# Graph attention on one core: the mask moves to the end, onto a word that holds both halves of a weight

## What is computed

```python
def _agnn(x, a, beta):
    x_norm = x / clip(norm(x, axis=-1), EPS)
    scores = beta[0] * (x_norm @ x_norm.T)
    scores = where(a > 0, scores, NEG_INF)
    attn = softmax(scores, axis=-1)
    return attn @ x

x = x + gnn(relu(layernorm(x)), adj, ...)
h = relu(layernorm(x))
h = leaky(_agnn(h, adj, beta1))
h = leaky(_agnn(h, adj, beta2))
out = x + h
```

## Time and profile before

| what | us |
|---|---|
| median of 3 runs | 1070.74 (1069.54 to 1072.2) |
| the profiled execution's own time | 1071.25 |
| its span, first to last instruction | 1069.7 |
| busy: TensorE, VectorE, ScalarE, GpSimd | 990.1, 929.9, 679.1, 34.0 |
| mean granted clock of TensorE | 0.972 of 2.4 GHz |

### The profile page before, as it was taken

One profiled execution on the slowest core, in us unless ns is written; L12 is line 12 of the kernel. 1 busy time (PEld: TensorE's weight loads), 2 busy tenths in 40 slices (PEclk: granted clock), 3 DMA queues, 4 the chain that ended last, 5 costly groups with the idle time before them and its releaser, 6 DMA issues.

```text
span 1069.7 us, 24266 instructions
## 1 busy us (share of the span) xinstructions
PE 990.1 (93%) x8672; PEld 665.3 (62%) x8672; DVE 929.9 (87%) x2276; ACT 679.1 (63%) x894; POOL 34.0 (3%) x31
## 2 busy tenths in 40 slices
PE   2889999999977699999999999969999999999995
PEld 2754444444445377777777777737777777777774
DVE  7692888888899979999999999958899899998996
ACT  2721112111234478889889898858888888888784
POOL 0000000000013500000000000000000000000000
PEclk9889999999998899999999999989999999999998
DMA  9228998888852346556555666616566665666600
GB/s 306 100 84 286 299 287 281 281 283 279 279 170 102 119 159 194 191 175 195 195 193 193 196 196 196 190 49 201 193 207 197 204 205 187 211 198 194 208 23 13
DMA packets 107231, 206.44 MB, mean 193 GB/s; under 512 B 3632, under 2 KB 8368, under 8 KB 107184
## 3 DMA queue, kind: packets, MB, share of 16 engines
q1 hardware_dynamic: 105536, 203.44, 59.2%
q0 software_dynamic: 640, 2.10, 0.6%
q10 hardware_dynamic: 1008, 0.33, 0.1%
HBM read 203.75 MB, written 2.10 MB: 192 GB/s over the span
## 4 chain that ended last, share of the span: by engine, by line
PE 54%; DVE 6%; issue 3%; ACT 1%; DVEq 0%; POOL 0%; ACTq 0%; POOLq 0%
PE s_ps L410 25%; PE acc_ps L426 10%; PE acc_ps L430 10%; PE acc_ps L428 9%; DVE h_all L1037 3%; DVE work L1030 1%; DVE t L1054 1%; DVE t L1062 1%; PE s_ps L351 0%; ACT work L638 0%; ACT t L677 0%; ACT t L660 0%; ACT h_all L645 0%; DVE set L906 0%; ACT t L666 0%
## 5 line engine op out<-in xcount | busy, mean ns | idle before, releaser
L638 ACT ACTIVATE work<-s_ps,beta_bias,beta_scale 128x1024 f32<-128x1024 f32 x256 | 307.1, 1200 | 91.3 <-PE s_ps L410 91.3
L1030 DVE SCALAR_TENSOR_TENSOR work<-ring,work 128x1024 f32<-128x1024 f32 x256 | 319.9, 1250 | 44.2 <-ACT work L638 41.7
L1037 DVE TENSOR_TENSOR h_all<-work,h_all 128x1024 f16<-128x1024 f32 x244 | 297.5, 1219 | 3.1 <-ACT h_all L645 2.8
L645 ACT ACTIVATE h_all<-work 128x1024 f16<-128x1024 f32 x256 | 268.3, 1048 | 33.6 <-DVE work L1030 33.2
L364 PE MATMUL acc_ps<-ring,set 128*128 128x512 f32 x512 | 225.6, 600 | 3.1 <-DVE set L888 3.1
L426 PE MATMUL acc_ps<-src,h_all 128*128 128x129 f16 x1024 | 186.2, 222 | 18.0 <-POOL h_all L276 9.9
L410 PE MATMUL s_ps<-set 128*128 (+1 forms) x768 | 187.5, 381 | 4.1 <-issue 3.1
L410 PE MATMUL s_ps<-xt 128*128 (+1 forms) x768 | 189.0, 384 | 0.8 <-DVE xt L906 0.4
L430 PE MATMUL acc_ps<-src,h_all 128*128 128x129 f16 x1024 | 186.3, 224 | 0.0
L428 PE MATMUL acc_ps<-src,h_all 128*128 128x128 f16 x1024 | 185.9, 222 | 0.0
L426 PE MATMUL acc_ps<-set,h_all 128*128 128x129 f16 x1024 | 182.4, 219 | 3.3 <-DVE h_all L1037 3.3
(11 more groups left out here) (186 smaller groups left out, 710.2 us busy)
## 6 DMA issues: line engine op xcount, KB each, us to landing
ring<-in_adj_t SPq DMA_DIRECT2D x192, 1024.0 KB, 5.3
x_sb<-in_x SPq DMA_DIRECT2D x4, 512.0 KB, 8.2
out<-x_sb POOLq DMA_DIRECT2D x8, 256.0 KB, 2.9
w<-in_layer ACTq DMA_DIRECT2D x2, 64.0 KB, 6.2
w<-in_embed ACTq DMA_DIRECT2D x1, 64.0 KB, 2.6
eb<-in_embed_bias ACTq DMA_DIRECT2D x1, 64.0 KB, 5.2
lb<-in_layer_bias ACTq DMA_DIRECT2D x1, 64.0 KB, 7.0
beta<-in_beta ACTq DMA_DIRECT2D x2, 0.5 KB, 6.4
```

The costliest lines, as they stand in the source:

```text
L638: nc.scalar.activation(e_ring[:, t % ER, :], s_ps[:, t % 2, :], ACT.Exp, bias=beta_bias[:, la:la + 1], scale=beta_scale[:, la:la + 1])\
L645: nc.scalar.activation(ph_ring[:, t % LAG, :], m_ring[:, t % LAG, :], ACT.Copy)\
L1030: V.scalar_tensor_tensor(m_ring[:, t % LAG, :], ring[:, k, half_tile:half_tile + SB, :] .rearrange("p b i -> p (b i)"), 0.0, e_ring[:, t % ...
L1037: V.tensor_tensor(pl_ring[:, t % LAG, :], m_ring[:, t % LAG, :], ph_ring[:, t % LAG, :], ALU.subtract).then_inc(pl_done[la], n)
```

## The change

The order of the four passes becomes exponential, high half, low half, mask. The high half is rounded from the unmasked exponential, the low half is the unmasked exponential minus it, and both are written into one 32-bit word, the low half into its lower 16 bits and the high half into its upper. The mask then multiplies that word, read as a float32, by 0 or 1, in place, which keeps or clears both halves at once. There are WR = 8 places for words (`halves` is the f16 view of one, in which neighbours of the same half stand two elements apart); `m_ring` and the two rings of halves are gone. `e_ring` keeps its two places, and its place is free once `p_lo` has read it. LAG is 5. VectorE does `p_lo(t-1)` and then `mask(t-2)`. On the shifted path the mask stays in front, as `mask_e`. The diff, cut to its core:

```diff
-    LAG = 4
+    LAG = 5
+    WR = 8
...
-        m_ring = work[:, ER * SB * CH:(ER + LAG) * SB * CH].rearrange("p (r n) -> p r n", r=LAG)
+        w_low = h_all[:, :].rearrange("p (r n) -> p r n", r=WR // 2)
+        w_high = work[:, ER * SB * CH:(ER + WR // 2) * SB * CH].rearrange("p (r n) -> p r n", r=WR // 2)
+        words = [(w_low, w_high)[i * 2 // WR][:, i % (WR // 2), :] for i in range(WR)]
+        halves = [w.bitcast(f16).rearrange("p (n s) -> p s n", s=2) for w in words]
+        WORD_LO, WORD_HI = 0, 1
...
                 for t in range(PAUSES):
                     pool.wait_ge(ph_done[0], t + 1)
-                    wait(pool, pv_done[0], t + 1 - LAG)
-                    pool.tensor_tensor(pl_ring[:, t % LAG, :], m_ring[:, t % LAG, :], ph_ring[:, t % LAG, :],
-                                       ALU.subtract).then_inc(pl_early, 1)
+                    pool.tensor_tensor(halves[t % WR][:, WORD_LO, :], e_ring[:, t % ER, :],
+                                       halves[t % WR][:, WORD_HI, :], ALU.subtract).then_inc(pl_early, 1)
...
-                wait_p_lo(pe, la, c * NS + (t + 1), joined)
+                pe.wait_ge(mask_done[la], c * NS + (t + 1))
+                w_hi, w_lo = halves[t % WR][:, WORD_HI, :], halves[t % WR][:, WORD_LO, :]
...
-                        last = nc.tensor.matmul(acc_ps[:, b, 0:PW], pl_ring[:, t % LAG, col],
+                        last = nc.tensor.matmul(acc_ps[:, b, 0:PW], w_lo[:, col],
                                                 src[la][:, jb, F:AW], start=False, stop=jb == NB - 1)
...
                 act.wait_ge(s_done[la], c * NS + (t + 1))
-                wait(act, mask_done[la], c * NS + (t + 1 - ER))
+                wait_p_lo(act, la, c * NS + (t + 1 - ER), joined)
                 nc.scalar.activation(e_ring[:, t % ER, :], s_ps[:, t % 2, :], ACT.Exp,
...
-            def p_hi(la, c, t):
-                act.wait_ge(mask_done[la], c * NS + (t + 1))
-                wait(act, pv_done[la], c * NS + (t + 1 - LAG))
-                nc.scalar.activation(ph_ring[:, t % LAG, :], m_ring[:, t % LAG, :], ACT.Copy)\
+            def p_hi(la, c, t, shifted):
+                act.wait_ge(e_masked[la] if shifted else exp_done[la], c * NS + (t + 1))
+                wait(act, pv_done[la], c * NS + (t + 1 - WR))
+                nc.scalar.activation(halves[t % WR][:, WORD_HI, :], e_ring[:, t % ER, :], ACT.Copy)\
                     .then_inc(ph_done[la], 1)
...
-                V.scalar_tensor_tensor(m_ring[:, t % LAG, :], ring[:, k, half_tile:half_tile + SB, :]
-                                       .rearrange("p b i -> p (b i)"), 0.0, e_ring[:, t % ER, :],
-                                       ALU.is_gt, ALU.mult).then_inc(mask_done[la], 1)
...
+            def mask(la, c, t, joined=False):
+
+                wait_p_lo(dve, la, c * NS + (t + 1), joined)
+                w = words[t % WR]
+                V.scalar_tensor_tensor(w, mask_in(la, c, t), 0.0, w, ALU.is_gt, ALU.mult).then_inc(mask_done[la], 1)
+
+            def p_lo(la, c, t, shifted, n=1):
+
                 dve.wait_ge(ph_done[la], c * NS + (t + 1))
-                wait(dve, pv_done[la], c * NS + (t + 1 - LAG))
-                V.tensor_tensor(pl_ring[:, t % LAG, :], m_ring[:, t % LAG, :], ph_ring[:, t % LAG, :],
-                                ALU.subtract).then_inc(pl_done[la], n)
+                V.tensor_tensor(halves[t % WR][:, WORD_LO, :], e_ring[:, t % ER, :], halves[t % WR][:, WORD_HI, :],
+                                ALU.subtract).then_inc(mask_done[la] if shifted else pl_done[la], n)
...
-                    mask(la, c, t, t0 > 0)
-                    norm_parts = range(4 * (t - LAG - 5), min(4 * (t - LAG - 4), NORM_PARTS))\
+                        mask_e(la, c, t)
+                    norm_parts = range(5 * (t - LAG - 5), min(5 * (t - LAG - 4), NORM_PARTS))\
                         if between and t >= LAG + 5 else ()
...
                     elif not first:
-                        p_lo(la, c - 1, NS - 1)
+                        p_lo(la, c - 1, NS - 1, shifted)
+                    if not shifted:
+                        if t > 1:
+                            mask(la, c, t - 2, t0 > 0)
+                        elif not first:
+                            mask(la, c - 1, NS - 2 + t)
...
             def between(i):
 
-                mask(0, 0, i, True)
+                if i > 1:
+                    mask(0, 0, i - 2, True)
...
-                p_lo(la, NC - 1, NS - 1)
+                p_lo(la, NC - 1, NS - 1, shifted)
+                if not shifted:
+                    mask(la, NC - 1, NS - 2)
+                    mask(la, NC - 1, NS - 1)
```

More of the change, by code:

```diff
@@ L76, in build @@
         xt = [xt0, set1_h[:, 0:2 * N].rearrange("p (s n) -> p s n", s=2)]
-        work = sb("work", [P, (ER + LAG) * SB * CH])
+        work = sb("work", [P, (ER + WR // 2) * SB * CH])
         e_ring = work[:, 0:ER * SB * CH].rearrange("p (r n) -> p r n", r=ER)
-        m_ring = work[:, ER * SB * CH:(ER + LAG) * SB * CH].rearrange("p (r n) -> p r n", r=LAG)
+        w_low = h_all[:, :].rearrange("p (r n) -> p r n", r=WR // 2)
[3 more added lines that the diff above has]
+        WORD_LO, WORD_HI = 0, 1
         adj_rows = work[:, 0:N]
@@ L174, in build @@
         mask_done = [sem(f"mask_done{i}") for i in range(2)]
+        e_masked = [sem(f"e_masked{i}") for i in range(2)]
         ph_done = [sem(f"ph_done{i}") for i in range(2)]
@@ L212, in __call__, with wait_p_lo @@
                 self.eng.wait_ge(self.s, self.base + self.n)
-        def wait_p_lo(eng, la, n, joined):
+        def wait_p_lo(eng, la, n, joined=False):
             if joined and n <= PAUSES:
@@ L415, in scores, with weighted_sum @@
                 last.then_inc(s_done[la], 1)
-            def weighted_sum(la, c, t, joined=False):
-                wait_p_lo(pe, la, c * NS + (t + 1), joined)
+            def weighted_sum(la, c, t):
+                pe.wait_ge(mask_done[la], c * NS + (t + 1))
+                w_hi, w_lo = halves[t % WR][:, WORD_HI, :], halves[t % WR][:, WORD_LO, :]
                 if t == 0:
@@ L466, in chunk @@
                     if t >= LAG:
-                        weighted_sum(la, c, t - LAG, joined)
+                        weighted_sum(la, c, t - LAG)
                     elif t >= TAIL[la] and not first:
@@ L481, in chunk @@
                 for t in range(TAIL[la]):
-                    weighted_sum(la, c, NS - LAG + t, joined)
+                    weighted_sum(la, c, NS - LAG + t)
                 if first:
@@ L628, in _, with exps @@
             asks_gnn = start + NC * ASKS_CHUNK
-            def exps(la, c, t, shifted):
+            def exps(la, c, t, shifted, joined=False):
                 if shifted:
@@ L689, in chunk @@
                         split_columns(1, c - 1, slot_ps)
-                    exps(la, c, t, shifted)
+                    exps(la, c, t, shifted, t0 > 0)
                     if la == 0 and not first and t == NS - 3:
@@ L695, in chunk @@
                     if t:
-                        p_hi(la, c, t - 1)
+                        p_hi(la, c, t - 1, shifted)
                     elif not first:
-                        p_hi(la, c - 1, NS - 1)
+                        p_hi(la, c - 1, NS - 1, shifted)
                     if not first and t == LAG:
@@ L708, in between @@
             def between(i):
-                exps(0, 0, i + 1, False)
+                exps(0, 0, i + 1, False, True)
                 if i >= 0:
-                    p_hi(0, 0, i)
+                    p_hi(0, 0, i, False)
                 if i == 1:
@@ L727, in attention @@
                     chunk(la, c, False, shifted)
-                p_hi(la, NC - 1, NS - 1)
+                p_hi(la, NC - 1, NS - 1, shifted)
                 sums_leave(la, NC - 1)
@@ L1022, in clamp, with mask_in, mask_e @@
                                 ALU.mult, ALU.min).then_inc(clamped[la], 1)
[L1024 removed]
+            def mask_in(la, c, t):
                 k, half_tile = t * SB // TB, t * SB % TB
[L1026 removed]
                 if half_tile == 0:
                     dve.wait_ge(tile_in[k], 16 * c + (tile_base[la] + 16))
[L1029 to L1034 removed]
+                return ring[:, k, half_tile:half_tile + SB, :].rearrange("p b i -> p (b i)")
+            def mask_e(la, c, t):
+                dve.wait_ge(exp_done[la], c * NS + (t + 1))
+                e = e_ring[:, t % ER, :]
+                V.scalar_tensor_tensor(e, mask_in(la, c, t), 0.0, e, ALU.is_gt, ALU.mult).then_inc(e_masked[la], 1)
+            def mask(la, c, t, joined=False):
[3 more added lines that the diff above has]
+            def p_lo(la, c, t, shifted, n=1):
                 dve.wait_ge(ph_done[la], c * NS + (t + 1))
[L1036 to L1038 removed]
+                V.tensor_tensor(halves[t % WR][:, WORD_LO, :], e_ring[:, t % ER, :], halves[t % WR][:, WORD_HI, :],
+                                ALU.subtract).then_inc(mask_done[la] if shifted else pl_done[la], n)
             def averages(la, c):
```

14 lines of the change are left out of this document (5 added, 9 removed).

## The result

The changed kernel takes 1389.8 us, the median of 4 runs (1389.05 to 1392.91); the kernel before took 1071.1 beside it. The ratio is 1.298, with a 95% interval of 1.296 to 1.301. Forecast were 1277 us and a range of 1256 to 1326: the direction was right, the size was not, and the time lies above the range. The profiled execution took 1389.05 us with a span of 1387.5, 317.8 more than before (1069.7).

A forecast was written before the change was run, and what follows sets the result against it. TensorE was taken to bound the kernel before, a closed loop through exponential, high half and low half after. 1071.25 + 96.0 (first attention) + 100.7 (second) + 2 + 1 (joined tiles' chunk) + 6 (ends) = 1277 us, range 1256 to 1326.

The forecast's parts named there:

- What bounds the kernel: Before the change TensorE sets the pace, 2.68 us a tile, VectorE close behind; a shorter path wins only small waits.
- the buffer of the exponential: With two places, the exponential waits for the low half of t-2, closing a loop: 3.45 us a tile against 2.68.
- What no row shows, a half word at every second place: Stepped passes on ScalarE and VectorE: bounds 0 to +0.98 us a turn; low end taken, no cost.
- The handoffs: Gaps between the loop's passes: overlap of 0.10 us, then 0.04 and 0.04; 0.03 either way in 238 turns, ±7.
- Chunk extras: Per chunk: 0.5 us in both attentions, 1.2 more and 0.6 at chunk ends in the first, 0.3 in the second.
- the forecast of TensorE's clock: TensorE stands idle 0.77 us a tile, yet its granted clock was expected to stay at 2.4 GHz (1.00).
- The joined first tiles: GpSimd does low halves there; its 4.45 us loop, eleven turns or 49 us, stays hidden in 58.8; +2 us, bounds ±6.
- The two ends: Behind the last high half VectorE does more passes: about +3 us at each end, +6 together.
- The strided passes are slow: Rival: stepped high or low halves cost more, +0.49 us a turn giving about 1394 us; chance 9%.
- The strided weight loads make TensorE the bound: Rival: weight loads pace x1.9, a tile takes 3.94 us, +0.49 over the loop, about 1394 us; chance 7%.
- Only a third place would open the loop: For the exponential's loop: no deeper word ring or longer lag opens it, only a third place for the exponential.
- The loop's own bounds: Range of the loop as computed, 1258 to 1300 us: joined stage ±6, handoffs ±7, chunk extras ±6; chance 77%.

The follow-up runs named there:

- The wait alone: Kernel before, with only the exponential's wait changed: tile t also waits for the low half of tile t-2; 1333.6 us, ratio 1.246.
- the order alone: Changed kernel with each tile's high half directly behind its own exponential on ScalarE, stepped half words and two places kept; 1086.7 us, ratio 1.016.
- the second experiment: Changed kernel with each half filling one contiguous part of its word's place, so no access steps over an element; 1288.0 us, ratio 1.204.
- the high half first: Changed kernel with the high half directly behind its own exponential: stepped 1086.7 us, ratio 1.016; with contiguous halves 1065.8 us, ratio 0.994.

## Why the prediction missed, point by point

**What bounds the kernel, and the buffer of the exponential: right.** The releaser of the exponential, its idle time (1.43 us a turn, 361 in all), TensorE's 73% at clock 1.00 in the steady stretch with its waits on the mask are as forecast. The wait alone, in the kernel before, made it slow; the order alone took 95% of the loss back.

**What no row shows, a half word at every second place: this step failed.** I took the low end of its bounds, no cost, on an argument about neighbouring words. Measured on 1024 elements, stepped against contiguous (the second experiment): ScalarE's high half 1.05 to 1.35 us, VectorE's low half 1.22 to 1.30 or 1.35, mean 0.105 more. That is 0.405 us a turn, 96 us over 237 turns. The true value lay between the two ends that stood in the text, 0 and 0.98, a little below the half way to which the rival gave 9%. The rule that I leaned on (the Trainium skill, Vector Engine (DVE) Microarchitecture Reference, section 5.2, full rate for runs of adjacent four-byte words) holds here only to 7 or 11%, on VectorE. It speaks of no half words and not of ScalarE's writes; the larger part of the cost is there.

**The handoffs: too small.** The three of the loop were put at -0.10, 0.04 and 0.04 (exponential to high half, to low half, to exponential); measured are -0.09, 0.03 and 0.10, so 0.06 a turn, 14 us. The last 0.04 was read from a high half released by VectorE, whose rows give 0.03; for an exponential released by it no row stood in the trace of before. The bound of 0.03 either way did not hold it.

**Chunk extras: the mechanism right, two small terms too many.** In the first attention one turn a chunk is 4.4 us (0.5 more, `sums_leave`) and one is 5.1 (1.2 more, `normalised`), in the second one is 4.4, all as forecast. The 0.6 at the chunk's end and the 0.3 for VectorE's longest slot do not appear; instead one single turn of 5.9 us does in each attention. So 2 us less than forecast in the first, and 0.3 less in the second. These two turns come where the forecast of TensorE's clock failed. The one in the first attention begins at 708.09; busy time there, in the view of windows:

```profile
708.00:712.00 4.00, 3.15 (x28) 2.76 (x27) 3.13 (x4) 2.45 (x2) 0.00 (x0) 0.50 0.47 182
```

The granted clock is 0.50, the lower of the two levels (1.2 of 2.4 GHz). The products go by every 0.11 us instead of 0.058, and the exponential waits 3.48 us for the scores. In the second attention the clock is 0.50 as well (926 to 928), and the turn also waits for the column sums (4.35 us in the kernel before). Between 390 and 688 us of the kernel before the clock was 1.00. In the changed kernel it falls at four chunk ends of the first attention, and only here did a turn grow. Before it fell TensorE was busy 2.85 of 4 us (700 to 704), much as in the steady stretch, where the clock stayed; so what makes it fall isn't shown.

**The joined first tiles: not hidden.** The loop through GpSimd was put at 4.45 us a turn and thought covered. Two slips met there. What I called tiles 0 to 12 are tiles 1 to 13, twelve steps in 58.8 us. And GpSimd's low half with a step takes longer than its 2202 ns of the earlier trace rows; its groups after:

```profile
L279 POOL TENSOR_TENSOR h_all<-work,h_all 128x1024 f16<-128x1024 f32 x8 | 20.9, 2616 | 269.7 <-ACT h_all L648 269.7
L279 POOL TENSOR_TENSOR work<-work 128x1024 f16<-128x1024 f32 x4 | 10.1, 2530 | 12.7 <-ACT work L648 12.7
```

The twelve steps now take 64.7 us (309.04 to 373.76), 5.9 more, inside the bound of 6. They begin 2.3 earlier, and with 0.8 behind them the part is 4.4 longer, forecast at 3. With contiguous halves the same steps take 58.2 (310.82 to 369.05), so what is no longer hidden goes with the step, although GpSimd's half is above 2202 ns there too (2289 and 2446). The two ends cost 8.8 where 6 were allowed.

**The rivals.** "The strided passes are slow" came true within the loop, at 0.405 of its 0.49. "The strided weight loads make TensorE the bound" gave the same 1394 us and is refuted by rows: a stepped load takes what a contiguous one did (100 ns), a product still goes by every 0.058 us, from 1103.26 to 1104.65 for 24 of them. The group of the loads, then TensorE by time:

```profile
L429 PEld LDWEIGHTS acc_ps<-set,work 128*128 128x128 f16 x512 | 51.4, 100 | 94.1 <-DVE work L1043 93.7
```

```profile
1103.26 0.23 PE L429 MATMUL acc_ps<-set,h_all 128*128 128x129 f16 x1 [1.05 <-DVE h_all L1043]
...
1104.65 1.46 PE L412 MATMUL s_ps<-set 128*128 x6
```

Of the two rules in the table "Weight-path perf modes" (the Trainium skill, TensorE: Matmul & The Clock Gate) the trace agrees with the one that allows strided columns.

**"Only a third place would open the loop": wrong.** Turning two instructions of ScalarE opened it wholly, without memory; the third place, as built here, opened two thirds.

**The range.** 112 us too low is mostly one unknown times 237. The text gave its ends as 0 and 0.98 us, and then let the range reach 0.2. (The loop's own bounds, 6, 7 and 6, add up to 1258 to 1296, not 1300.) With 16% on two rivals that both ended at 1394, a range to 1400 would have cost little.

## What to carry to other kernels

When a buffer's release moves to a later pass, follow the waits through each engine's order: an instruction that waits for another engine's pass, which itself waits for the instruction directly ahead, closes a loop, and every pass in it adds its whole length to the tile; turning two instructions can be worth more than a buffer. A pass that is a few per cent longer costs nothing beside a full engine and everything inside such a loop. An access pattern that no row shows gets both ends of its price multiplied by the number of turns, and the range keeps them.

## What the runs showed of the hardware that was not expected

- A float16 result with a step of two elements costs ScalarE 0.30 us on 1024 elements a partition (1.05 to 1.35, 29%), VectorE, which reads one stepped operand and writes another, 0.08 to 0.13 on 1.22, GpSimd 0.33 and 0.08 on the 2.29 and 2.45 that its low half takes in the changed kernel with contiguous halves (words in `h_all` and in `work`). With the high half first it is 0.22 and nothing. Which half of the word it is makes no difference.
- VectorE's stepped pass takes 1304 ns with the word in `h_all` and 1351 with it in `work`, where the exponential lies too; contiguous both are 1225. Sharing the tensor is not the reason: in the run with a third place, where the exponential lies in `e_third`, they are 1325 and 1369. The reason is open.
- TensorE reads stepped weights at no cost that shows: 100 ns a load, 58 ns a product, and a full 50 of 50 us.
- From the end of VectorE's low half to an exponential that waits for it 0.09 to 0.11 us go by where an instruction of ScalarE's queue lies between, 0.03 to 0.05 where none does; from ScalarE's high half to the low half it is 0.02 to 0.04.
- TensorE's granted clock, 1.00 in the steady stretches, fell to 0.50 at single chunk ends of the changed kernel (708 to 712), and a turn of 3.9 us became one of 5.9. Why is open.
